# Taking 17 products of zeros out of the first stage of a fused attention and mixture-of-experts kernel

## The reference, cut to what matters

```python
x = x + layernorm(attention(layernorm(x)))     # x: (2, 2048, 128) float32
x = x + layernorm(moe(layernorm(x)))

# attention has no softmax, 16 heads of width 8: all of it is products
dots = (p @ metric_h) @ p.T ; nudged = dots @ p      # p = x @ projection_h
out = nudged.reshape(B, W, C) @ mixer_w.T + mixer_b

# moe: 8 experts, top 2 by logits + beta, weight sigmoid(logit), plus one shared expert
logits = xt @ gate_w.T ; idx = top_k(logits + beta, 2)
combined = sum over the two experts of (silu(xt @ g_e) * (xt @ u_e)) @ d_e * weight
return combined + shared_out
```

## Time and profile before

| | |
|---|---|
| median of 3 runs | 247.47 us (245.0 to 247.66) |
| the profiled execution's own time | 245.01 us |
| its span, first to last instruction | 242.9 us |
| outside the span | 2.1 us |
| PE busy | 223.1 us, 92% |
| DVE busy | 167.0 us, 69% |
| ACT busy | 134.8 us, 56% |
| POOL busy | 162.1 us, 67% |
| mean granted TensorE clock | 0.977 of full |

### The profile page before, as it was taken

The page is one execution under the profiler, slowest core; times in us unless marked ns, Lnnn a source line. Parts: engine busy times, 40 slices in busy tenths (PEclk is TensorE's granted clock), DMA queues, the critical chain, the costliest instruction groups (busy, mean ns, idle before and its releaser), DMA issues.

```text
span 242.9 us, 5859 instructions
## 1 busy us (share of the span) xinstructions
PE 223.1 (92%) x1270; PEld 160.9 (66%) x1270; DVE 167.0 (69%) x796; ACT 134.8 (56%) x502; POOL 162.1 (67%) x210
## 2 busy tenths in 40 slices
PE   7999887889999979999799999999999999989970
PEld 2868574545545335368688888888888888887340
DVE  3967989787999998868555656656655555511795
ACT  2848585474666753655455555555555555503761
POOL 7965757777777777777777666666665766660730
PEclk9999998879999999999999999999999999999996
DMA  6799001111111113641233233323233232108963
GB/s 178 201 316 275 0 22 49 56 56 45 57 60 45 57 56 91 166 125 58 78 98 106 81 100 88 93 69 110 69 99 80 81 89 78 47 22 280 395 235 131
DMA packets 28315, 26.34 MB, mean 108 GB/s; under 512 B 7014, under 2 KB 22259, under 8 KB 28288
## 3 DMA queue, kind: packets, MB, share of 16 engines
q1 hardware_dynamic: 22448, 15.38, 22.7%
q0 software_dynamic: 4320, 8.53, 9.9%
q10 hardware_dynamic: 1520, 2.10, 2.4%
HBM read 14.77 MB, written 11.68 MB: 109 GB/s over the span
## 4 chain that ended last, share of the span: by engine, by line
PE 69%; DVE 13%; DMA 5%; ACT 4%; issue 3%; POOL 2%; POOLq 1%; SPq 0%; ACTq 0%; DVEq 0%
PE bank L1388 12%; PE bank L1279 9%; PE bank L1361 6%; PE bank L1363 6%; PE bank L1362 6%; PE bank L1379 6%; PE bank L1149 4%; PE bank L1342 3%; PE bank L1291 3%; PE bank L1253 3%; PE bank L1165 2%; DMA xnT<-expert_results 2%; PE bank L1207 2%; ACT work L603 2%; DVE X L1136 2%
## 5 line engine op out<-in xcount | busy, mean ns | idle before, releaser
L545 POOL DMA_INDIRECT expert_results<-eo,rowt x71 | 69.8, 983 | 32.0 <-issue 29.2
L527 POOL DMA_INDIRECT expert_rows<-src,slot x64 | 63.4, 991 | 21.2 <-issue 18.6
L722 ACT ACTIVATE work<-bank 128x256 f32<-128x256 f32 x71 | 27.3, 384 | 46.0 <-PE bank L1363 45.9
L1388 PE MATMUL bank<-down,work 128*128 x284 | 44.1, 278 | 0.4 <-ACT work L729 0.2
L1085 DVE TENSOR_TENSOR work<-work,bank 128x256 f32<-128x256 f32 x48 | 20.2, 421 | 27.8 <-ACT work L722 27.2
L1388 PEld LDWEIGHTS bank<-down,work 128*128 128x128 f32 x284 | 37.3, 192 | 1.6 <-issue 0.8
L1361 PE MATMUL bank<-gu_hi,rh 128*128 x71 | 34.3, 484 | 0.3 <-DVE rl L1077 0.3
L1279 PE MATMUL bank<-xT,gu_f 128*128 128x512 f32 x64 | 33.5, 646 | 0.0
L729 ACT ACTIVATE work<-bank 128x256 f32<-128x256 f32 x71 | 27.8, 392 | 1.0 <-PE bank L1379 1.0
L1363 PE MATMUL bank<-gu_hi,rl 128*128 x71 | 28.1, 395 | 0.0
L1362 PE MATMUL bank<-gu_lo,rh 128*128 x71 | 27.9, 392 | 0.0
(11 more groups left out here) (195 smaller groups left out, 445.6 us busy)
## 6 DMA issues: line engine op xcount, KB each, us to landing
rowt<-expert_rows SPq DMA_DIRECT2D x71, 66.0 KB, 1.9
X<-n_L_attn_in_sequence_bwc SPq DMA_DIRECT2D x8, 256.0 KB, 3.9
X<-expert_results SPq DMA_DIRECT2D x8, 256.0 KB, 6.7
xnT<-expert_results ACTq DMA_DIRECT2D x8, 256.0 KB, 7.3
out<-X SPq DMA_DIRECT2D x7, 256.0 KB, 3.5
expert_results<-eo,rowt POOLq DMA_INDIRECT x71, 2.3
gu_f<-in_L_ffn_gate_proj_w SPq DMA_DIRECT2D x1, 1024.0 KB, 7.3
gu_f<-in_L_ffn_up_proj_w SPq DMA_DIRECT2D x1, 1024.0 KB, 10.0
```

The costliest lines, as they stand in the source:

```text
L527: nc.gpsimd.indirect_dma_start(rows_d, bass.IndirectOffsetOnAxis(ap=slot[i % SRC][:, n // TOPK, n % TOPK:n % TOPK + 1], axis=0), src[i % S ...
L545: nc.gpsimd.indirect_dma_start(res_d, bass.IndirectOffsetOnAxis(ap=rowt[v][:, P:P + 1].bitcast(U32), axis=0), eo[v][:], None, bounds_check ...
L722: nc.scalar.activation(sgate[v % 2], gu_ps[v % 2][:, 0:M], ACT.Silu).then_inc(slot_silu, 1)
L1388: last = mm(y_ps[w], hidT[w][:, a, :], down[:, e, a, :], start=a == 0, stop=a == MC - 1)
```

## The change

Six of the seven calls of `warm_up` are taken out: 2 products between links 1 and 2 of entry 0, 2 between `router_weights` and link 3, 3 between `gram(4)` and `gram(5)`, 2 after `attention(2)`, 3 between `rows_T(0)` and `logits(0)`, and 5 between `logits(0)` and `prefix(0)`. That is 17 products. The 18 at the head stay, and nothing else on any engine is changed.

```diff
             link(0, 1, S_sb[0][:], Wf)
-            warm_up(2)
             link(0, 2, Wf, T1[0][:])
...
             router_weights()
-            warm_up(2)
             link(0, 3, Gm[0][:], mixT[:])
...
             gram(4)
-            warm_up(3, 1)
             gram(5)
             attention(2)
-            warm_up(2, 1)
...
             rows_T(0)
-            warm_up(3, 1)
             logits(0)
-            warm_up(5, 1)
             pe.wait_ge(route_consts, 1)
             prefix(0)
```

## The result

Over 22 executions each, the changed kernel took 249.08 us in the median (247.08 to 252.54) and the kernel before 246.62 us (244.65 to 250.04). The ratio is 1.0101, with an interval from 1.0075 to 1.0126: slower by about 2.5 us. The forecast was +0.75 us with a range of 245.3 to 250.3; the sign and the range hold, and the change was three times as large as forecast.

The account below looks back on a forecast made before the run. Until about 120 us POOL's scatter queue and the PE, ACT and DVE loop bound the kernel side by side, then PE until about 213. Sum -0.1 + 0.05 + 0.8 = +0.75 us, 247.47 to 248.2 us, range 245.3 to 250.3.

Parts of the forecast that it names:

- The zeros on the path: At the removed products on PE: taking them out gains 0 to 0.4 us, taken as 0.1.
- The fall at about 30.4 us: Near the start of prefix(0): clock at half until about 33.8 us, making the loop 1.4 us late, bounds 0 to 1.7.
- What POOL sees of it: At POOL's scatter queue: margins of step 2 between 0.12 and 1.06 us let 0.34 to 1.28 through, taken as 0.8.
- What the loop gives back: At the earlier half-speed stretches from 40.4 and 50.7 us: shifts taken as 0, with 0.3 back and 0.7 forth.
- The handover: First stage to second: PE's 1.27 us lead leaves 0.13 of the loop's 1.4, so POOL's 0.8 decides.
- The first scatter: Start of POOL's queue: moves by only 0.05 us, starting near 32.8 us.
- the rival with an early fall: Before the first scatter: clock falls earlier, doubling attention(0) or logits(0), end at 249.8 to 250.3 us; chance 0.18.
- The doubling of the logits: At logits(0), within the early-fall case: a fall ahead of them adds at most 0.9 us.
- The signs that the prediction named: In the changed profile: half clock from 29 to 32 us, logits and mask within 0.2, 64th scatter 0.3 to 1.3 later.
- How many falls: In the first stage: one more fall of the clock to half, near prefix(0), lasting about 3.4 us.
- slower by over 1%: Outcome for the whole kernel: slower than the kernel before by more than 1% (2.5 us); chance 0.15.
- The estimate of under 2.4 us: Whole kernel: the skill's ramp penalty, below 1% of a typical span, gives under 2.4 us; not used in the sum.

Follow-up runs that it names:

- t1_all: The kernel before, cut to end behind step 1 of the first stage, with all 17 products at full width; 47.07 us.
- t3_tiny: The cut kernel of t1_all with all 17 products in place but 8 columns wide instead of 512; 49.49 us.
- e2: The changed kernel with 4 of the 17 products back, those between the links of entry 0; 295.91 us, ratio 1.0141 to the kernel before.
- e9: The same kernel as e2, run again: 4 of the 17 products back, between the links of entry 0; 297.46 us against 294.0 for the kernel before.
- t2: The cut kernel of t1_all with none of the 17 products; 49.77 us.
- the three cut kernels: The kernel ended behind step 1, with all 17 products, none, or all 17 but 8 columns wide; 47.07, 49.77 and 49.49 us.
- e1_router: The changed kernel with 8 of the 17 products back, 3 before and 5 behind logits(0); 296.9 us, ratio 1.0079 to the kernel before.

## Why the prediction was right, and what was sized wrong

*The zeros on the path, taken at 0.1 us.* Nothing was gained: the removed products left waits of 0.37, 0.69 and 2.08 us in the changed kernel, and t1_all and t3_tiny start `prefix(0)` together. The chain's 2.71 us for them were a cover, not a cost.

*The fall at about 30.4 us and its 1.4 us.* Right in place (30.7 us in t3_tiny, 32.1 in the changed kernel) and price: 1.44 us at the destinations of step 1. The working behind the price was loose: the 1.39 us of the earlier trace rows is what 2.8 us at half cost, the part from 51.32 to 54.1 us that met products, not all 3.4. In three profiles (e2, e9, t2) it lasted twice as long, which I had not allowed for.

*What POOL sees of it: 0.8 of 1.4 us. This term was sized too small.* The margin of step 2 was taken between 0.12 and 1.06 us, according to how much of the first scatter's 0.94 us lies between release and start. The changed kernel has three scatters that wait in a running queue: `slot` ends at 44.42, 58.14 and 70.21 us, and they start at 45.20, 58.92 and 70.99. That is 0.78 us each time. So the margin of step 2 in the kernel before was 53.86 - 52.80 - 0.78 = 0.28 us, and of one fall 1.4 - 0.28 = 1.1 us reach the end rather than 0.8.

*What the loop gives back, taken at 0, with 0.7 forth in the range. This failed in size as well.* In the changed kernel the later stretches at half grew from 3.4 and 3.4 us to 10.1 and 6.6. The lateness of `slot` against the earlier trace rows goes from 0.81 us in step 0 to 2.42 and 5.34 us in steps 1 and 2. Of the last growth, 2.9 us, most is the stretch from 42.3 to 52.4 us, into which three pairs of the shared expert's products and attention(4) fall. What makes that stretch longer in one execution and not in another I can only argue: the first delay moves the thin places of the loop. The nine runs of full kernels do not settle it.

*The handover.* The forecast let PE's lead of 1.27 us absorb its share. The lead stayed, 1.16 us: POOL's queue was late by as much as the loop. Right that the POOL path decides.

*The first scatter, taken as fixed.* Right in t3_tiny (31.69 us for `slot` against 31.68) and in e2_links, wrong in the profile of the changed kernel, where the rival with an early fall came in: attention(0) at half speed, priced at 0.7, and 0.81 late less 0.09 of a later start = 0.72 us. It had a chance of 0.18; the fall at 18 us was in three of seven profiles without the links' products, so by these few it was given too little. The doubling of the logits, 0.9 us, was not seen in the changed kernel, where they ran at full clock and took 1.06 us as before; where the fall began inside them they took longer, 1.35 us in e9_links_again and 1.22 in t2_none, so a part of that price is real.

*The signs that the prediction named.* In the profile of the changed kernel most of them did not come. Logits and mask of step 0 are 0.81 and 0.80 us late, not within 0.2; the wait for `slot` is there, but the 64th scatter is 7.36 us later, not 0.3 to 1.3; PE's wait at the handover was 1.16 us, hardly shorter than 1.27. The first scatter moved by 0.81 us, and over 0.5 was named as a sign that the prediction is wrong. The half-speed stretch that should begin between 29 and 32 us began at 32.1, and the Gram products behind it did follow each other half as fast, one every 0.64 us instead of 0.33. This execution is the early-fall rival and not the forecast; the forecast's picture is that of t3_tiny. Of the executions nearer to the median there is no profile.

*How many falls. This is the largest of the sizes that were wrong.* The forecast gave the changed kernel one more stretch of 3.4 us at half. The mean granted clock of every execution says how long it was at half in all, span x 2 x (1 - clock). By this the profile of the kernel before has 11.2 us, 6.8 in its two stretches and most of the rest at the end of the span, where PE is idle. The median of the 22 executions of the changed kernel is 21.6 us; the median of 11 executions of the kernel before that ran beside the three cut kernels is 12.8. So the typical execution spent some 9 us more at half, not 3.4. In the cut kernels it is 3.4 us in t1_all, 13.7 in t2_none and 13.2 in t3_tiny, where the profile of t3_tiny, with one fall ahead of 40 us, has 9.7. At most half of such time can be lost. That 2.5 us are lost and not 4.5 says that some of it met PE while it waited, or was held by the margins behind; which of the two was not measured.

So the mechanism was as forecast, and so were place and price of one fall. The forecast execution, one fall and a margin of 0.28, comes to 1.1 us; no run of the full kernel shows it by itself. The other 1.4 us of the median are the falls that I had left to a rival and to the range; this division of the median is worked out, not measured. That 248.2 us lies within 0.9 of 249.08 is in part luck: it was counted from 247.47, the median of three executions, and 22 executions have 246.62. The ratio of 1.0101 lies on the border of "slower by over 1%", which had 0.15.

*What the Trainium skill says.* That activity releases the throttled clock (the Trainium skill, "TensorE: Matmul & The Clock Gate", Part 1) spoke against the change and was right: eight products at full width keep 1.00 where eight narrow ones give 0.50. The same part says that the number of slow products at the start of one kernel differs from run to run. No run here shows that for the start, but later falls vary in the same way: one and the same kernel has its fall at 29.4 us in e2_links and at 28.6 in e9_links_again. The estimate of under 2.4 us that the prediction took from that part is a figure for the ramp at the start; what the later falls cost here is 2.46 us, or 1.8 to 3.1 by the interval, so it is neither met nor refuted.

## What to carry to other kernels

Idle time that filler work occupies is free only if nothing depends on the engine having been busy: before taking filler out, look at what the engine runs next and what that costs at half clock, 1.44 us for one fall here. A chain of waits names filler as the path whenever it ends together with the true releaser; the test is whether the follower has another wait that ends just ahead of its start, here by 0.04 to 0.16 us. And a queue that runs without a gap is a second path beside the one that feeds it: its margin at each step, release latency (0.78 us here) subtracted, says how much of a delay is absorbed.

## What the runs showed that I had not expected

- A transpose on PE also slows with the clock: 0.27 us in the Gram steps at full clock, 0.42 us at half in the changed kernel's `gram(6)`, where the product beside it goes from 0.39 to 0.63 us. The timeline of PE there:

```profile
32.89 0.42 PE L1171 MATMUL bank<-ident,xn_all 128*128 128x128 f32 x1
...
35.77 0.27 PE L1171 MATMUL bank<-ident,xn_all 128*128 128x128 f32 x1
```

- The same program took 293 to 295 us on one chip and 246.6 us on another, with equal durations of the single instructions (DVE's product at line 1085 has a mean of 421 ns in the changed kernel's profile and 420 in e1_router's), and stalls of 1 us and more between them.
